# An attention block with a dense branch: key splits on GpSimd, first queries placed by 0/1 matmuls, value products among the first pairs, and the last output finished on VectorE in column halves

## What is computed

```python
xn = layernorm(x)
q = relu(xn @ Wq.T + bq); k = relu(keys @ Wk.T + bk); v = relu(values @ Wv.T + bv)
score = einsum('bhsd,bhtd->bhst', heads(q), heads(k)) / sqrt(16)
a = einsum('bhst,bhtd->bhsd', softmax(score), heads(v))
a = transpose(a, (0, 1, 3, 2)).reshape(xn.shape)
y = clip(xn @ sign(Wf).T * scale + bias, -100, 100)
out = x + (a + xn) + y
```

## Time and profile before

| | |
|---|---|
| median of 3 runs | 2848.66 us (2847.84 to 2852.46) |
| the profiled execution | 2850.59 us, of which the span of the trace is 2848.8 |
| PE, ACT, DVE, POOL busy | 97%, 86%, 82%, 33% of the span |
| start, up to the first half-step's first score | 105 us |
| steady half-steps | 105 to 2823 us |
| end, behind the last weighted sum | 2825 to 2849 us |

### The profile page before, as it was taken

How to read it: one execution, slowest core, us unless ns; L and a number is a source line. 1 busy time by engine, 2 the same in 40 slices (tenths; PEclk the granted TensorE clock), 3 DMA queues, 4 the chain that set the end, 5 groups by cost and what they waited for, 6 DMA issues and landing times.

```text
span 2848.8 us, 61155 instructions
## 1 busy us (share of the span) xinstructions
PE 2770.7 (97%) x17860; PEld 1149.8 (40%) x17860; DVE 2337.4 (82%) x4578; ACT 2450.2 (86%) x2949; POOL 938.4 (33%) x845
## 2 busy tenths in 40 slices
PE   8899999999999999999999999999999999999996
PEld 4434444443444434444443444434444443444331
DVE  6788888888888888888888888888888888888940
ACT  4688888888888888888888888888888888888996
POOL 4304334242343314333242343314333242343001
PEclk8699999999999999999999999999999999999998
DMA  7111121121221121121121221121121121211111
GB/s 142 60 40 55 65 70 36 56 70 55 65 70 52 40 70 55 65 66 33 62 69 55 65 66 49 47 70 55 65 64 35 62 68 56 65 62 37 48 55 38
DMA packets 78637, 167.74 MB, mean 59 GB/s; under 512 B 28548, under 2 KB 32647, under 8 KB 76327
## 3 DMA queue, kind: packets, MB, share of 16 engines
q1 hardware_dynamic: 78374, 164.19, 19.2%
HBM read 36.71 MB, written 17.83 MB: 19 GB/s over the span
## 4 chain that ended last, share of the span: by engine, by line
PE 79%; issue 10%; DVE 7%; ACT 2%; POOL 1%; DVEq 0%; DMA 0%; POOLq 0%; ACTq 0%
PE value_ps L611 30%; PE ring L633 28%; PE score_ps L597 13%; DVE mx L959 5%; ACT probs L806 2%; PE score_ps L677 1%; PE score_ps L662 1%; PE score_ps L679 1%; PE score_ps L666 1%; PE score_ps L664 1%; PE ring L720 1%; POOL fin L1097 1%; PE score_ps L715 0%; DVE excess L934 0%; PE ring L700 0%
## 5 line engine op out<-in xcount | busy, mean ns | idle before, releaser
L806 ACT ACTIVATE probs<-score_ps 128x1024 f32<-128x1024 f32 x2048 | 1992.3, 1024 | 236.1 <-PE score_ps L597 229.9
L959 DVE TENSOR_REDUCE mx<-ring 128x1 f32<-128x512 f32 x2952 | 1900.1, 684 | 248.8 <-PE ring L633 224.5
L633 PE MATMUL ring<-kstack,qstack 48*128 48x512 f32 x3444 | 1168.4, 467 | 16.7 <-DVE mx L959 3.1
L611 PE MATMUL value_ps<-probs,vones 128*32 128x512 f32 x8192 | 1092.3, 605 | 1.1 <-ACT taken L813 0.4
L633 PEld LDWEIGHTS ring<-kstack,qstack 48*128 48x128 f32 x3444 | 490.1, 184 | 1071.0 <-DVE mx L959 1034.3
L597 PE MATMUL score_ps<-qstack,kstack 51*128 51x512 f32 x4096 | 814.1, 416 | 13.8 <-ACT probs L806 4.5
L934 DVE CUSTOM_DVE_ANT_0 excess<-ring,excess 128x512 f32<-128x512 f32 x512 | 353.1, 690 | 136.7 <-PE ring L633 119.1
L1097 POOL TENSOR_TENSOR dense<-dense,affine 128x512 f32<-128x512 f32 x128 | 164.4, 1284 | 866.7 <-ACT dense L856 865.2
L597 PEld LDWEIGHTS score_ps<-qstack,kstack 51*128 51x128 f32 x4096 | 393.6, 186 | 132.1 <-ACT probs L806 70.5
L822 ACT ACTIVATE excess<-ring 128x512 f32<-128x512 f32 x492 | 294.0, 597 | 1.4 <-PE ring L633 1.2
L611 PEld LDWEIGHTS value_ps<-probs,vones 128*32 128x32 f32 x8192 | 161.5, 108 | 320.7 <-issue 289.1
(11 more groups left out here) (93 smaller groups left out, 1417.2 us busy)
## 6 DMA issues: line engine op xcount, KB each, us to landing
qstack<-parts SPq DMA_DIRECT2D x768, 64.0 KB, 2.5
fin<-taken SPq DMA_DIRECT2D x256, 128.0 KB, 2.9
xin<-x SPq DMA_DIRECT2D x16, 1024.0 KB, 5.1
base_cur<-base_new SPq DMA_DIRECT2D x16, 1024.0 KB, 5.3
fin<-recip SPq DMA_DIRECT2D x32, 512.0 KB
out<-fin SPq DMA_DIRECT2D x32, 512.0 KB, 2.6
qstack<-proj SPq DMA_DIRECT2D x256, 12.0 KB
kstack<-base_cur SPq DMA_DIRECT2D x16, 128.0 KB, 6.0
```

The source lines that it names most:

```text
L611: mm = pe.matmul(value_ps[h4 * 32:(h4 + 1) * 32, :], vones[:, 2 * tp + c, hh * HALF + side * PAIRS + 2 * g + j, :, :], probs[:, q % 2 * GR ...
L633: pe.matmul(ps[:, :], qstack[nh][rows, pair, st * P:(st + 1) * P], keys, start=True, stop=True).then_inc(s_mm, 1)
L806: nc.scalar.activation(probs[:, q % 2 * GROUP + u % GROUP, :], score_ps[src][:, :], ACT.Exp, scale=EXP_SCALE).then_inc(s_probs, 1)
L959: nc.vector.tensor_reduce(most, src[:, :], AX.X, ALU.max).then_inc(s_mx, 1)
```

## The change

1. **Front of the start.** `split_keys` moves from DVE to GpSimd (high and low part, both channel halves), and the second channel half's difference too; DVE keeps the first difference, now computed from `key_proj` into `taken`. The two transposed tiles of the first batch get a buffer each (`proj`, `dense`) instead of sharing one. The ±1 weights are made earlier on DVE.
2. **First queries.** The 12 DMAs that place queries of pairs 0 to 15 are replaced by 8 matmuls with 0/1 matrices (`picks`, made on DVE from `ident`), 4 banks, copied into `qstack` by ACT (2) and DVE (2). SP's list is 12 DMAs shorter.
3. **Values, scale and dense.** The 8 value products, the scale and bias rows and dense jobs 0 and 1 no longer stand in front of the pairs. Scale stands at pair 1, dense jobs at pairs 2, 4, 9 and 14 (before: two in front, the others at 5 and 9), one value product in front of each of pairs 32 to 39. They go through `value_ps`; ACT takes `affine`.
4. **Last output.** For the last half batch alone, pack, DRAM trip and `finish` are left out. DVE takes the reciprocal of the gathered sums where they lie (128x512), multiplies and adds, once for each half of the columns, and each half is written out by itself.

```diff
+        START_SCALE, START_DENSE = 1, {2: 0, 4: 1, 9: 2, 14: 3}
+        START_VALUES = len(START) - NTC
...
             sp.wait_ge(s_ones, 4)
+            sp.wait_ge(s_ks, 1)
             stack_keys(0, 1, s_kd)
             sp.wait_ge(s_split, 2)
-            for g in range(2):
-                load_queries(0, 0, g)
-            sp.wait_ge(s_kx, 6)
+            load_queries(0, 0, 1)
+            sp.wait_ge(s_ky, 3)
             stack_keys(1, 1, s_ke)
...
+            def select_queries(n):
+                a, i, to = SELECT_JOBS[n]
+                ps = bank(-1, to, (s_selA, s_selV)[i], 0, a + 1)
+                for term in range(2):
+                    mm = pe.matmul(ps[:, :], picks[:, i, term, :, :, :, :].rearrange("p s h k d -> p (s h k d)"),
+                                   parts_r[:, term, a * BANK:(a + 1) * BANK], start=(term == 0), stop=(term == 1))
...
+            pe.wait_ge(s_ir, 5)
+            for n in range(2 * NA):
+                if n % 2 == 0:
+                    pe.wait_ge(s_split, n // 2 + 1)
+                select_queries(n)
...
+                if j == START_SCALE:
+                    project_scale()
                 if j in START_DENSE:
                     do_job(0, 0, "dense", START_DENSE[j], None, None)
+                if j >= START_VALUES:
+                    project_values(j - START_VALUES)
...
+            def finish_end(a):
+                cols = slice(a * BANK, (a + 1) * BANK)
+                dve.wait_ge(s_gather[a], NB * 4 * 32)
+                nc.vector.reciprocal(fin[:, 1, cols], fin[:, 1, cols]).then_inc(s_end, 1)
+                dve.wait_ge(s_end, 3 * a + 1)
+                nc.vector.tensor_tensor(fin[:, 0, cols], fin[:, 0, cols], fin[:, 1, cols], ALU.mult).then_inc(s_end, 1)
...
+            def split_keys(oc):
+                keys = key_proj[:, oc, :, :].rearrange("p a t -> p (a t)")
+                pool.wait_ge(s_kr, NTH * (oc + 1))
+                tt(key_parts_r[0][:, oc, :], keys, C_ONE.broadcast_to([P, T]), ALU.mult).then_inc(s_kc, 1)
+                pool.wait_ge(s_kc, oc + 1)
+                tt(key_parts_r[1][:, oc, :], keys, key_parts[0][:, oc, :], ALU.subtract).then_inc(s_ks, 1)
```

More of the change, by code:

```diff
@@ L142, in attention_block @@
         diff_parts = [qstack[1][:, k, :].rearrange("p (o t) -> p o t", o=2) for k in range(2)]
+        key_diff = taken
+        first_turned = [proj, dense]
         key_parts_r = [part.bitcast(FP32R) for part in key_parts]
@@ L521, in half_step @@
                     gather(*last, 3)
+                if last and not (now or att):
+                    result = out[NB - 1].rearrange("(f p j) c -> f p (j c)", f=2, p=P)[1]
+                    for a in range(NA):
+                        cols = slice(a * BANK, (a + 1) * BANK)
+                        sp.wait_ge(s_end, 3 * a + 3)
+                        sp.dma_start(result[:, cols], fin[:, 1, cols]).then_inc(s_out, 16)
+                    return
+                if last:
                     pack_sums(*last)
-                if last:
                     spread_reciprocals(*last)
@@ L691, in project_keys, with project_scale, project_values @@
                 mm.then_inc(s_kp, 1)
[L693 to L702, removed]
+            def select_queries(n):
[4 more added lines that the diff above has]
+                                   parts_r[:, term, a * BANK:(a + 1) * BANK], start=(term == 0), stop=(term == 1))
+                mm.then_inc(s_sel, 1)
+            def project_scale():
+                ps = tile(0, None, s_ws, 0, 1)
+                pe.matmul(ps[:, 0:H], ones_row, scale_row, start=True, stop=True)
+                pe.matmul(ps[:, H:2 * H], ones_row, bias_row, start=True, stop=True).then_inc(s_sc, 1)
+            def project_values(tc):
+                if tc % 2 == 0:
+                    tile(0, None, s_vr, 0, tc // 2 + 1)
+                dst = value_ps[:, tc % 2 * H:(tc % 2 + 1) * H]
+                pe.matmul(dst, ones_row, bv_row, start=True, stop=False)
+                for ic in range(IC):
+                    mm = pe.matmul(dst, vals_sb[:, ic, tc * P:(tc + 1) * P], wv_sb[:, ic, :],
+                                   start=False, stop=(ic == IC - 1))
+                if tc % 2 == 1:
+                    mm.then_inc(s_vp, 1)
             def start_maxima(j, at):
@@ L880, in _ @@
                 take_keys(n)
-            for k in range(NA):
-                take_job(-1, 1, "turn", k, None, k)
+            for a in range(NA):
+                take_first_turned(a)
             for n in range(2, 4):
                 take_keys(n)
-            for n, src in VALUE_JOBS[:1]:
-                take_values(n, src)
             act.wait_ge(s_wq, 32)
@@ L889, in _ @@
                 take_job(-1, 1, "project", a, 0, a)
+            for n in range(0, 2 * NA, 2):
+                take_selected(n)
             act.wait_ge(s_split, 2)
@@ L1053, in _ @@
             for a in range(NA):
+                normalise_first(a)
+            split_first_difference()
+            for a in range(NA):
+                split_first_turned(a)
+            for a in range(NA):
                 split_first_queries(a)
-            split_keys(1)
-            dve.wait_ge(s_sc, 1)
-            nc.vector.tensor_copy(affine[:, :, :], ring[SCALE_BANK][:, :].rearrange("p (k c) -> p k c", c=H)
-                                  ).then_inc(s_ws, 1)
+            for n in range(1, 2 * NA, 2):
+                copy_selected(n)
             dve.wait_ge(s_ones, 4)
@@ L1084, in half_step @@
                                              b * 2 * REDS + made(hh, TILES - 1))
-                    if last and d == RECIP_UNIT // 2:
+                    if last and (now or att) and d == RECIP_UNIT // 2:
                         reciprocals(*last)
@@ L1091, in _ @@
             run(dve, half_step)
+            for a in range(NA):
+                finish_end(a)
         @block.gpsimd
@@ L1234, in _ @@
             root(-1)
+            for oc in range(2):
+                split_keys(oc)
+            split_second_difference()
             pool.wait_ge(s_xn, NA)
+            pool.wait_ge(s_kx, 3)
             pool.wait_ge(s_ws, 1)
-            pool.wait_ge(s_kx, 6)
             for a in range(NA):
@@ L1253, in half_step @@
                         split_turned(b, a)
-                if last:
+                if last and (now or att):
                     finish(*last)
```

116 lines of the change are left out of this document (72 added, 44 removed).

## The result

The changed kernel took 2859.08 us (median of 13 executions, 2854.99 to 2861.78), the kernel before 2850.24 beside it (13 as well, 12 of them between 2847.84 and 2852.46, one at 3193.63). The ratio is 1.0032, with a 95% interval of 1.0025 to 1.004: slower by 0.3%, where I had forecast 2838 and gave a slower kernel 4 in 100.

A forecast was written before the change was run, and what follows sets the result against it. PE was taken as busy 97%, so only the start (pairs bound by DVE) and the end could move: 2850.6 + 1.1 (-10.6 + 4.3 + 7.4) - 11.7 = 2840.0, less 1.9 is 2838 us; 8-in-10 range 2830 to 2844.

The forecast's parts named there:

- 1.25 pairs low and 6.75 full: Pairs 32 to 39 with value products: clock soon rises from 1.2 GHz to full, 21.2 us in all, +7.4.
- the sum for full clock: Pairs 32 to 39: a value product and four matmuls take 2.3 us a pair at full clock, 18.4 for eight.
- Rival B: Pairs 32 to 39: values at low clock throughout, 32 to 37 us, +18 to +23; time 2849 to 2854; chance 0.10.
- Rival C: Pairs 32 to 39: low clock, and PE also waits for ACT to empty `value_ps`, +27; time 2858; chance 0.04.
- the front: Stretch up to pair 0: pair 0 starts at 33.5 us in place of 44.09, -10.6.
- hidden by the six differences ahead on SP: Front: GpSimd's key split, from about 15.8 to 20.6, is done before SP needs it at 22.4.
- this list starts 1.9 earlier: Front: SP's list of key DMAs starts 1.9 us earlier, as DVE skips two passes over 1024 keys.
- the end of the queries: Front: selecting matmuls, second projection and a copy end near 31 us, ahead of the keys at 33.5.
- Rival D: Front: GpSimd's splits run slower beside DVE, keys are late, pair 0 starts at 37; time 2841.5; chance 0.07.
- Scale and dense among the pairs: Among the pairs: four dense jobs and scale cost DVE 10.5 us against 6.2 before, +4.3.
- Behind the pairs: From the end of the pairs to the transposes: these follow DVE's end by 7.1 us as before, 0.
- The end: Behind the last gather: DVE finishes the last output, with a reciprocal of 3.3 us, -11.7.

The follow-up runs named there:

- block: The changed kernel with all eight value products standing together ahead of pair 32, none between the pairs: 2860.56 us, ratio 1.0045 to the kernel before.
- warm-up run: The changed kernel with all eight value products together ahead of pair 32, behind 16 added matmuls whose results are thrown away: 2875.18 us (one execution).

## Why the prediction was wrong, and where it was right

**The step that failed most: "1.25 pairs low and 6.75 full".** I had no row of value products at 1.2 GHz and took the clock to rise in them since it had stayed full under them in the earlier trace rows. Staying and rising are not the same: the clock stayed at 0.50 for 35 us under fully booked PE (changed kernel) and 25 us (block), and at 1.00 under the same work entered warm (warm-up run). What decided was the one-row matmul, shown twice: left out, or widened by zero rows, the clock rose. With it widened, the eight pairs took 20.4 us; the sum for full clock was sound and its premise was not. The Trainium skill ("TensorE: Matmul & The Clock Gate", Part 1, What's actually happening) has the throttle set by how busy PE has recently been. By that rule PE, booked 35.00 of 35 us, would have been released, and the trace does not agree.

The low clock of 58 to 91 us in the earlier trace rows spoke against my step already, and I gave it 0.10. Rival B had the right outcome and nearly the right price (32 to 37 us, measured 34.8), for a reason that was not the right one: it put the low clock down to the 48-row matmuls, and held the 128 rows of the values against itself. The stuck clock that it cites from the Trainium skill (same page, Seeing it yourself) is one of a quarter, K=1/4; here the granted clock was 0.50, so the level does not agree. Rival C's wait for `value_ps` did not come: PE has no idle time from 91 to 126 us. That C's time, 2858, lies next to the measured 2859.08 is luck: its 27 us stand for 21.0 there and for most of the front's 7.5, which it did not have. (By my own sum the kernel turns slower once a pair costs 4.7 us, and not 4.9 as I wrote: 2854.4 - 2830.7 + 13.8 = 37.5 us for eight.)

**The second: "hidden by the six differences ahead on SP".** I priced GpSimd's split by whether its own result is late. It was not: the first was done at 22.01, and SP came to its DMA at 26.60. The cost lay in DVE, which had the queries' chain, and was held 9.2 us in six instructions. So the step "this list starts 1.9 earlier" failed as well: SP's list waits for DVE's difference and began at 22.58, where 18.5 was forecast. And the end of the queries that I had put near 31 became the bound: PE waited for `xnT_low` until 31.02, its matmuls were slower behind that wait (8.9 us from there to the end of the second projection, for 7.6 with the splits on DVE), and pair 0 came at 40.94. Undone, pair 0 came at 34.32, for a forecast of 33.5, waiting for keys as I had written.

Rival D saw the two engines side by side but asked only whether GpSimd would slow down (its second subtraction did, 3.23 for 2.41). And each rival stood by itself, at 0.10 and 0.07: no sum had B and D together, which is what came. The Trainium skill ("GPSIMD Engine Reference", 1. Specifications) would have asked the right question. It says that GpSimd's SBUF interfaces are shared with VectorE, with contention for VectorE instructions in a 2-port mode or with two SBUF inputs. The trace agrees: the two-input subtractions were held, and so were the casts, whose second 512 elements cost half of the subtraction's (0.26 us, from 0.43 to 0.69, against 0.54, from 0.69 to 1.23), while `join`, which reads one input from PSUM, kept its 0.69 beside GpSimd in the pairs. The timeline of the changed kernel, DVE and GpSimd:

```profile
52.76 0.69 DVE L988 CUSTOM_DVE_ANT_0 excess<-ring,excess 128x512 f32<-128x512 f32 x1 [2.61 <-PE score_ps L755]
...
53.99 0.69 DVE L988 CUSTOM_DVE_ANT_0 probs<-ring,probs 128x512 f32<-128x512 f32 x1
...
53.72 1.28 POOL L1172 TENSOR_TENSOR dense<-dense,affine 128x512 f32<-128x512 f32 x1
```

**Right.** Scale and dense among the pairs: +4.8 for +4.3. DVE's waits for them were 0.78, 1.58 and three times 2.61, 10.2 us for the 10.5 of the forecast. That the sum fits so well is in part luck: the clock for the first job was not full (0.50 from 44 to 47 us), and in the block's run, where it was 1.00 for the 10 us behind pair 0, the same stretch took 47.5 us, +1.8. Behind the pairs: +0.1 for 0. The end: -11.65 for -11.7 in the profile, -10.8 between medians; the reciprocal of 512 took 3.35 for 3.3, worked out from a fixed part and a rate, against the estimate of 4.3 us that I had worked out from the repeat count of 8 in the Trainium skill ("VectorE: DVE Perf Modes", First, the fixed hardware budget); the trace does not agree with that estimate.

**Not forecast.** The steady part was 2.5 us shorter, which no step of the change explains: it is 2707.5 to 2714.3 us in the profiles of kernels that don't differ there. Open is also the 16 us gap in one run. The wide bias and the splits on DVE together fall 3.3 us short of the sum of their gains (2838.71 for 2859.08 - 16.8 - 6.9 = 2835.4), but that lies within the interval of the run.

## What to carry to other kernels

Price work that is moved to an idle engine by what it does to its neighbours as well as by its own time: look at each instruction of the other engine that will run beside it, and ask where it reads from. Before moving matmuls to a stretch with a low clock, find a row in which the clock rises under just such matmuls; one in which it stays high does not show that it will rise. And run the parts of a change one by one: here one part of four, the end, held nearly all of the gain, and two (values among the pairs, splits on GpSimd) took back more than it gave.

## What the runs showed of the hardware that I had not expected

- One-row matmuls among 128-row ones keep the granted clock from rising: 0.50 for 35 us with PE fully booked, against a rise after about 1.3 pairs once the same matmul had 128 rows, 127 of them zeros. They do not bring a full clock down (1.00 for 14 us).
- A VectorE cast from SBUF, or a subtraction of two SBUF tiles, that starts beside a GpSimd instruction ends a little less than its usual duration behind it: 2.00 us in place of 0.43, 2.72 in place of 0.69. One-input GpSimd instructions do it as well, each for less (1.41 for 0.69). A `join`, with one input from PSUM, kept its 0.69.
- PE can stand idle for 16.16 us in a steady loop without a wait in the profile, in one run of a kernel.
